# Two post-norm transformer layers on one core: weight loads on another queue, two sets of split parts, row maxima through an fp32 transpose, and new orders

## The reference, cut to what matters

```python
x = _layernorm(x + _L0_attn_ref(x, L0_attn_w_project, L0_attn_w_out), axis=-1)
x = _layernorm(x + _L0_ffn_ref(x, L0_ffn_gate_w, ..., L0_ffn_down_s), axis=-1)
x = _layernorm(x + _L1_attn_ref(x, L1_attn_Wq, ..., L1_attn_bo), axis=-1)
x = _layernorm(x + _L1_ffn_ref(x, L1_ffn_W_up, L1_ffn_W_gate, L1_ffn_W_down), axis=-1)
# attention, 16 heads of 16, causal:
att = jnp.einsum('bhqd,bhkd->bhqk', q, k) / math.sqrt(HEAD_DIM)
att = jax.nn.softmax(jnp.where(causal, -1e9, att), axis=-1)
out = jnp.einsum('bhqk,bhkd->bhqd', att, v)
# expert (ternary_quant: scale = mean|W|, clip(round(W/scale), -1, 1) * scale):
hidden = jax.nn.silu(x @ wu.T) * (x @ wg.T);  y = hidden @ wd.T
```

## Time and profile before

| | |
|---|---|
| median of 3 runs | 284.59 us |
| profiled execution | 287.4 us, of which the span is 285.7 |
| TensorE busy | 253.5 us (89%), mean granted clock 0.933 |
| VectorE busy | 222.5 us (78%) |
| GpSimd busy | 162.1 us (57%) |
| ScalarE busy | 153.6 us (54%) |

### The profile page before, as it was taken

The page is one execution under the profiler, slowest core; times in us unless marked ns, Lnnn a source line. Parts: engine busy times, 40 slices in busy tenths (PEclk is TensorE's granted clock), DMA queues, the critical chain, the costliest instruction groups (busy, mean ns, idle before and its releaser), DMA issues.

```text
span 285.7 us, 6810 instructions
## 1 busy us (share of the span) xinstructions
PE 253.5 (89%) x2396; PEld 221.3 (77%) x2396; DVE 222.5 (78%) x833; ACT 153.6 (54%) x284; POOL 162.1 (57%) x171
## 2 busy tenths in 40 slices
PE   1997646899999999999999898798999999999991
PEld 1897323467789999989999796676779888999980
DVE  1746999888967466853888999999998987888674
ACT  3634315567773524593634447657777765425440
POOL 9966235785550416443293796685651796645371
PEclk9999755569999999999999999799999999999996
DMA  6997556182000000016173029135021000010101
GB/s 212 319 247 195 170 158 175 37 262 79 6 0 2 2 0 5 0 35 191 44 201 127 1 61 262 51 87 139 7 83 67 5 0 2 2 39 0 39 1 73
DMA packets 18898, 24.18 MB, mean 85 GB/s; under 512 B 2480, under 2 KB 17328, under 8 KB 18224
## 3 DMA queue, kind: packets, MB, share of 16 engines
q1 hardware_dynamic: 18048, 22.95, 27.8%
q10 hardware_dynamic: 816, 0.79, 1.0%
HBM read 9.97 MB, written 1.05 MB: 39 GB/s over the span
## 4 chain that ended last, share of the span: by engine, by line
PE 55%; DVE 14%; DMA 8%; issue 7%; POOL 7%; SPq 4%; ACT 4%; POOLq 0%; DVEq 0%; ACTq 0%
PE pair L484 7%; PE pair L485 6%; PE pair L486 6%; PE pair L565 6%; PE pair L632 5%; PE pair L633 4%; SPq L461 4%; PE pair L548 4%; POOL k_stack L981 4%; PE pair L529 3%; PE pair L568 2%; PE pair L575 2%; DMA raw<-f0gu 2%; DMA raw<-f0dn 2%; PE pair L654 2%
## 5 line engine op out<-in xcount | busy, mean ns | idle before, releaser
L1013 POOL TENSOR_SCALAR_AFFINE_SELECT probs<-probs 128x512 f32<-128x512 f32 x64 | 42.6, 671 | 40.3 <-ACT probs L721 39.2
L1029 POOL TENSOR_TENSOR hidden<-hf,hidden 128x512 fp32r<-128x512 f32 x28 | 36.1, 1290 | 42.8 <-ACT hidden L763 42.7
L873 DVE CUSTOM_DVE_ANT_0 masked<-pair,mask 128x256 bf16<-128x256 f32 x128 | 53.5, 418 | 7.5 <-PE pair L530 7.3
L721 ACT ACTIVATE probs<-pair 128x768 f32<-128x768 f32 x64 | 49.2, 814 | 15.1 <-PE pair L550 12.9
L876 DVE CUSTOM_DVE_ANT_0 masked<-pair,mask 128x128 bf16<-128x128 f32 x128 | 36.4, 284 | 0.0
L936 DVE SCALAR_TENSOR_TENSOR hf<-th,pair 128x512 f32<-128x512 f32 x28 | 19.2, 685 | 20.2 <-ACT th L752 11.8
L529 PE MATMUL pair<-k_stack,q_stack 96*128 96x256 bf16 x128 | 30.7, 305 | 4.5 <-DVE row_max L876 2.3
L548 PE MATMUL pair<-q_stack,k_stack 98*128 98x256 bf16 x128 | 28.7, 294 | 4.4 <-DVE row_max L876 2.3
L763 ACT ACTIVATE hidden<-hf 128x512 fp32r<-128x512 f32 x28 | 17.7, 631 | 20.2 <-DVE hf L939 15.4
L484 PE MATMUL pair<-xT_hi,gu_hi 128*128 128x256 f32 x96 | 27.6, 288 | 1.0 <-DVE hf L939 1.0
L530 PE MATMUL pair<-k_stack,q_stack 96*128 96x128 bf16 x128 | 27.4, 239 | 0.0
(11 more groups left out here) (136 smaller groups left out, 844.0 us busy)
## 6 DMA issues: line engine op xcount, KB each, us to landing
q_stack<-q_part SPq DMA_DIRECT2D x48, 128.0 KB, 2.4
k_stack<-k_part SPq DMA_DIRECT2D x48, 128.0 KB, 2.5
raw<-f SPq DMA_DIRECT2D x3, 1024.0 KB, 5.4
raw<-f0gu SPq DMA_DIRECT2D x2, 768.0 KB, 5.9
x<-x_nat SPq DMA_DIRECT2D x1, 1024.0 KB, 8.1
raw<-a SPq DMA_DIRECT2D x1, 1024.0 KB, 5.0
out<-x SPq DMA_DIRECT2D x4, 256.0 KB, 2.2
probs<-x_tr SPq DMA_DIRECT2D x3, 256.0 KB, 5.9
```

The lines of the kernel that those rows point to most:

```text
L721: nc.scalar.activation(probs[(n - 1) % 4][:, :, :], place(key)[:, :, 0:T + P], ACT.Exp, scale=SC).then_inc(exp_done, 1)
L873: nc.vector.tensor_tensor_reduce(out=masked[:, j, 0:T], in0=o[:, 0:T], in1=mask[:, 0:T], scale=1.0, scalar=NEG, op0=ALU.add, op1=ALU.max, ...
L1013: pool.affine_select(out=diag, in_=diag, compare_op=ALU.is_ge, fill=0.0, base=0, pattern=[[0, 2], [0, 2], [1, P]], channel_multiplier=-1). ...
L1029: pool.tensor_tensor(hidden[(n - 1) % NHID][1][:, :, :], hf[n % 2][:, :].rearrange("p (a t) -> p a t", a=2), hidden[(n - 1) % NHID][0][:, ...
```

## The change

1. The -1 rows of the k stacks are written as fp32 words that each hold two bf16 values of -1.
2. SP's first loads are ordered anew, and the load of `x_nat` is issued behind batch 0's stack transfers. The seven later loads into `raw` become steps RAW on ScalarE, each with the wait it had on SP.
3. There are two sets of the q/k parts, taken in turn, so ScalarE waits only for the transfers of the batch before the last.
4. Row maxima: TensorE transposes `row_max` itself in fp32 (padded to 128 columns), ScalarE copies 16 rows as the high part, VectorE subtracts to get the low part, and SP writes them with two transfers (MX and ML) instead of one.
5. All five orders and the bank table are written anew, and `shift` is kept in `bo_b`.

```diff
+MINUS_PAIR = struct.unpack("<f", struct.pack("<I", 0xBF80BF80))[0]
...
 SYNC_STEPS = """
-    LOAD:001-2 LOAD:000 QK:000 PREPA:003 MID:000 LO:000 MID:001 QK:001 LO:001 QK:010 MID:010 QK:011 PREP0:001
+    LOAD:000-1 QK:000 MID:000 LO:000 QK:001 LO:001 MID:001 LOAD:002 QK:010 MID:010 QK:011 LO:010 QK:020-1 LO:011
...
-        part_of = [[sb(f"{name}_part{n}", [P, 2 * T], bf16) for n in range(3)] for name in "qk"]
+        part_of = [[[sb(f"{name}_part{n}_{m}", [P, 2 * T], bf16) for n in range(3)] for name in "qk"] for m in range(2)]
...
             load_a0(sp, 0)
-            for b in range(1, NB):
-                load_x(sp, b)
+            load_a0(sp, 1)
+            load_x(sp, 1)
+            load_a0(sp, 2)
+            load_x(sp, 2)
+            load_x(sp, 3)
             load_a0(sp, 3)
...
+                if step in ("MX", "ML"):
+                    n = nth("MX", l, b)
+                    row, done, part = (KP, maxT_hi_done, maxT_hi) if step == "MX" else (KP + 1, maxT_done, maxT_lo)
+                    sp.wait_ge(done, n)
+                    sp.dma_start(q_stack[nb_of(l, b) % SLOTS][row:row + 1, :, :].rearrange("p h t -> p (h t)"),
+                                 part[n % 2][:, :]).then_inc(max_rows[n % 2], 16)
...
                 if step == "MX":
-                    pe.wait_ge(max_split, nth("MX", l, b))
+                    pe.wait_ge(max_taken, 2 * nth("S", l, b, NS - 1))
...
-                        last = nc.tensor.matmul(o[:, qt * P:(qt + 1) * P], max_hl[:, qt, :],
-                                                ident_b[:, :], start=True, stop=True)
+                        last = nc.tensor.transpose(o[:, qt * P:(qt + 1) * P], row_max[b % 2][:, qt, :], ident[:, :])
...
         def _(act):
             load_x(act, 0)
-            load_a0(act, 1)
-            load_a0(act, 2)
...
+                if step == "RAW":
+                    if i == 0:
+                        act.wait_ge(wa0_lo, 4)
+                        act.dma_start(raw[:, 0:2 * W0], f0gu[:, 0, :]).then_inc(raw_in, 16)
+                    if i == 1:
+                        act.wait_ge(w_lo, 2)
+                        act.dma_start(raw[:, 0:2 * W0], f0gu[:, 1, :]).then_inc(raw_in, 16)
...
+                    if i == 4:
+                        act.wait_ge(w_lo, PREP0 + PREP1)
+                        act.dma_start(raw[:, :], f1[:, 0, :]).then_inc(raw_in, 16)
...
-                    for q in before_of(l, b):
-
+                    if nb_of(l, b) > 1:
+
+                        q = batches[nb_of(l, b) - 2]
                         act.wait_ge((q_stacked, k_stacked)[i][nb_of(*q) % SLOTS], stacked_by(*q))
...
-                    rm = row_max[b % 2]
-                    nc.vector.tensor_copy(max_hl[:, :, 0:H], rm[:, :, :]).then_inc(max_hi, 1)
-                    dve.wait_ge(max_hi, n)
-                    nc.vector.tensor_tensor(max_hl[:, :, H:2 * H], rm[:, :, :], max_hl[:, :, 0:H],
-                                            ALU.subtract).then_inc(max_split, 1)
+                    dve.wait_ge(maxT_hi_done, n)
+                    nc.vector.tensor_tensor(maxT_lo[n % 2][:, :], place(key)[0:H, 0:T], maxT_hi[n % 2][:, :],
+                                            ALU.subtract).then_inc(maxT_done, 1)
...
-                pool.memset(k_stack[n][KP:KP + 2, :, :], -1.0).then_inc(minus_rows, 1)
+                pool.memset(k_stack[n][KP:KP + 2, :, :].bitcast(fp32), MINUS_PAIR).then_inc(minus_rows, 1)
```

More of the change, by code:

```diff
@@ L221, in program @@
         ident = sb("ident", [P, P])
-        ident_b = sb("ident_b", [P, P], bf16)
         mask = sb("mask", [P, 384])
@@ L249, in program @@
         masked = sb("masked", [P, 2, T + P], bf16)
-        row_max = [sb(f"row_max{n}", [P, 2, H]) for n in range(2)]
-        max_hl = sb("max_hl", [P, 2, 4 * 2 * H], bf16)
-        maxT = sb("maxT", [2 * H, T], bf16)
+        row_max = [sb(f"row_max{n}", [P, 2, P]) for n in range(2)]
+        maxT_hi = [sb(f"maxT_hi{n}", [H, T], bf16) for n in range(2)]
+        maxT_lo = [sb(f"maxT_lo{n}", [H, T], bf16) for n in range(2)]
         probs_all = sb("probs", [P, 4 * 2 * (T + P)])
@@ L292, in program @@
         k_stacked = [sem(f"k_stacked{n}") for n in range(SLOTS)]
-        max_rows = sem("max_rows")
+        max_rows = [sem(f"max_rows{n}") for n in range(2)]
         stored = sem("stored")
@@ L696, in _ @@
                     act.wait_ge(qk_left, nth("SPLIT", l, b, i))
-                    nc.scalar.activation(part_of[i][1][:, :], left[i][:, :], ACT.Copy).then_inc(qk_mid, 1)
+                    nc.scalar.activation(part_of[nb_of(l, b) % 2][i][1][:, :], left[i][:, :], ACT.Copy).then_inc(qk_mid, 1)
                 if step == "V":
@@ L853, in _ @@
                         dve.wait_ge(qk_lo, k_ - 2)
-                    src, first = place(key), part_of[i][0]
+                    src, first = place(key), part_of[nb_of(l, b) % 2][i][0]
                     if l == 0:
@@ L865, in _ @@
                         dve.wait_ge(consts, 6)
+                    if i == 0 and nth("MX", l, b) > 2:
+                        dve.wait_ge(mx_mm, nth("MX", l, b) - 2)
                     for j in range(2):
@@ L980, in _ @@
             for n in range(SLOTS):
-                pool.memset(k_stack[n][KP:KP + 2, :, :], -1.0).then_inc(minus_rows, 1)
+                pool.memset(k_stack[n][KP:KP + 2, :, :].bitcast(fp32), MINUS_PAIR).then_inc(minus_rows, 1)
             pool.wait_ge(minus_rows, SLOTS)
             pool.memset(ones[:, :], 1.0).then_inc(consts, 1)
-            pool.memset(ident_b[:, :], 0.0).then_inc(pool_own, 1)
             pool.memset(minus_half[:, :], -0.5)
-            pool.memset(max_hl[:, :, 2 * H:4 * 2 * H], 0.0).then_inc(consts, 1)
+            for n in range(2):
+                pool.memset(row_max[n][:, :, H:P], 0.0).then_inc(consts, 1)
             pool.memset(ident[:, :], 0.0).then_inc(pool_own, 1)
             pool.memset(mask[:, :], 0.0).then_inc(pool_own, 1)
-            pool.wait_ge(pool_own, 3)
-            pool.affine_select(out=ident_b[:, :], in_=ident_b[:, :], compare_op=ALU.not_equal, fill=1.0, base=0,
-                               pattern=[[-1, P]], channel_multiplier=1).then_inc(consts, 1)
+            pool.wait_ge(pool_own, 2)
             pool.affine_select(out=ident[:, :], in_=ident[:, :], compare_op=ALU.not_equal, fill=1.0, base=0,
```

170 lines of the change are left out of this document (79 added, 91 removed), and 16 rows, old and new, of the table BANKS.

## The result

The changed kernel takes 295.39 us (294.1 to 298.0), the one before on the same chip 285.1 us (284.52 to 286.16): ratio 1.0337, 95% interval 1.0284 to 1.0391. I had forecast 279.1 and at most 285.5. The profiled execution took 296.58 us, 294.8 of it span.

The account below looks back on a forecast made before the run. VectorE was taken to set the pace to about 55 us, PE after it. Gains of 3.5 us in the start and 2.0 in layer 1, together 5.5, took 284.6 to 279.1 us, range 274.3 to 285.5.

Parts of the forecast that it names:

- -1 rows: GpSimd's start: memsets as fp32 pairs fall from 10.40 to 5.2 us, visible gain 2.3 us; 0 if time goes by bytes.
- x late: Start: x_nat's load issued behind batch 0's stacks costs nothing, as its reader comes tens of us later.
- Loads on ScalarE: Seven weight loads moved from SP cost ScalarE's queue about 0.6 us each, 4 in all; taken 0, bound 4.
- My rival: Slower: a layer-1 weight load in ScalarE's order delays batch (1,1)'s k split, PE idles 4 us; 288.1 us, chance 0.1.
- Batch 1's stacks: Start: 20 SP issues, 13 us, about 1 us of waits to 32.5, 2.5 us to land: there at 35.0.
- VectorE's 37.0: Start: VectorE begins batch 1's maxima at 37.0 against 38.31, 1.3 us earlier.
- My own sign for a wrong forecast: Start: the forecast is wrong if batch 1's stacks keep VectorE idle past 38 us.
- Row maxima: VectorE: 9.4 us of small operations removed, 8 subtractions of 0.41 added, 3.3 us; 6.1 saved, bounds 0.8 and 8.0.
- The clock: Start: PE's granted clock, which rose at 62.8 us, is back at 1.0 between 56 and 60.
- Layer 1: Less VectorE work and perhaps no half-clock stretch at 182 us: 2.0 us gained, bounds -3 and +4.
- The rule on issuing engines: Loads from another engine share 16 DMA engines, saving only issue time; cited for the rival without a lead, 283.6, chance 0.15.
- the small sum: Moving seven loads off SP is worth about seven issues of 0.6 us there and no faster landing.

Follow-up runs that it names:

- after_x_early: The changed kernel with SP issuing the x_nat load ahead of batch 0's stack transfers instead of behind them: 296.21 us, 1.0353 to the kernel before.
- after_queues_untied: The changed kernel with ScalarE's second gate/up load and SP's last k parts of batch 1 issued ahead of the waiting batch 2 k copy: 291.91 us, ratio 1.0149.
- after_light_loads: The changed kernel with layer 1's three feed-forward weight loads carrying 16 columns instead of 2048: 293.58 us, ratio 1.0259 to the kernel before.

## Why the prediction was wrong

- **-1 rows.** Size right: 5.28 us, taken 5.2. Their 2.3 us at S:000 came as 1.2 in the whole change; alone they moved the end by nothing that can be told. I had S:000 start at 22.7 behind ScalarE's copies. These and VectorE's subtraction were through by 21.4, but batch 0's stacks were not: SP had issued them by 17.86 (18.3 taken), the k transfers took 5.3 us in the median and not 2.5, and PE started S:000 at 23.24.
- **x late: nothing.** At the end it costs no more than early (after_x_early). But it fills the DMA engines beside batch 1's stacks, which I left out of their landing time.
- **Loads on ScalarE: taken 0.** Too low for the old orders (1.6% gained alone), and in the new orders a step failed here: I worked out when the first gate/up load goes out and never when the second does. It stands behind QK:021's copy, and that behind PE's 2.81 us stall for batch 0's stacks, three scores and 12 products at half clock: 28.13 us. I had ScalarE free of that wait; it stood 6.03 us for PE and 4.17 for the load. My rival said that ScalarE is in order and any of the seven waits could do it, and then priced only the one at 145 us, which did no harm (PE was busy 24.69 of 25 us in 150 to 175).
- **Batch 1's stacks: 35.0. This is the step that failed first.** I counted 20 issues and "about 1 us of waits". SP waited 1.9 us for QK:021 and was through these 20 at 34.1, not 32.5. One of the last, from 33.53, took 6.59 us to land, not 2.5: 40.1. Of the 5.1 us, 4.1 are the landing, which I had taken from the median of the earlier trace rows over the whole kernel, and 1.0 the queue. From there VectorE's 37.0 became 41.88. Why the landing was long is shown only in part: the DMA engines were full from 18 to 38 us (1.09 against 0.74), with `x_nat`, the slipped load and batch 2's parts in flight. With `x_nat` moved away the transfer took 4.30 us (after_x_early); the other two were never taken away by themselves. What is shown is that issuing batch 1's parts and the load ahead of the copy gives 1.9% back (after_queues_untied). My own sign for a wrong forecast, VectorE idle for these stacks past 38, came true.
- **Row maxima: 6.1 us saved.** A saving is there, if smaller (busy 4.0 us less when done alone; 7.8 in the whole change, beside other differences), and the subtraction takes 0.41 as estimated, all eight times. But I priced it as VectorE time and not as a link: PE, ScalarE, VectorE, SP and a transfer now follow one another, 2% slower and not faster. This is the second failed step.
- **The clock.** The long half-clock stretch does end sooner (56.4 against 62.8), as forecast. But it is no longer alone: there are three short ones, 6.8 + 6.7 + 6.8 us, each begun while PE stood idle (2.81, 2.65 and 1.93 us), where the kernel before had one of 3.5 at 182 us.
- **Layer 1: +2.0.** PE idles 4.82 us in 175 to 205 and not 3.39. The load at 175.29 goes out with batch (1,2)'s stacks behind it, some 0.8% (after_light_loads, not clear of its interval).
- **The rule on issuing engines** (the Trainium skill, DMA: Bandwidth & Descriptors, section Issuing engines are not separate DMA queues): loads issued by another engine share the same 16 DMA engines, so moving them saves issue time. The landings agree with the sharing: in the new orders a q stack transfer takes 5.7 us in the median with the loads on ScalarE and 5.1 with them on SP. At the end of the kernel the small sum held in one case of three: moving the seven loads alone gave 1.6%, about 4.5 us, where their issues on SP are some 4; in the new orders it is worth 2.0% (1.0543 against 1.0337), with the changed operations and the old orders nothing (1.0130 and 1.0137). So the issue time saved does not fix what the end gains; the order around the loads matters as well.

The sum of the parts closes within the intervals: 0.9844 for the loads, 2.0% for the maxima and 0.6% for the three others (0.5 - 0.3 + 0.4, each within its interval of nothing) make 1.010, measured 1.0137; the start's orders add 2.0%. Left open is why the new order behind the start, whose waits on PE are others, does no better and no worse than the old one.

## What to carry to other kernels

When instructions trade places, walk every in-order queue and ask what stands behind each waiting instruction, loads and DMA issues above all: one copy that waited 6 us for its product held back a weight load and the next batch's transfers, and moving those two past it was worth 1.9%. An operation that gets cheaper but now waits for two other engines has become a link: price the chain, not the busy time. And take a transfer's landing time from rows where the same neighbours are in flight.

## What the runs showed of the hardware

- A 128 KB transfer from SBUF to SBUF took 2.4 us to land in the median of the kernel before. With the DMA engines full (share 1.09 from 18 to 38 us) those of the changed kernel took up to 7.8 us, 6.59 in the chain. In layer 1 they took 6.1 us (q) and 4.9 (k) in the median beside a 1 MB load and 2.4 without it (after_light_loads). Which engine had issued the loads made little difference: 5.7 us with them on ScalarE, 5.1 with them on SP.
- GpSimd's memset goes by elements and not bytes: 4096 bf16 in 3.47 us each, the same bytes as 2048 fp32 in 1.76 (three took 10.40 and 5.28).
- At 70.2 and 186.1 us PE was granted half clock for 6.7 and 6.8 us, and both times the fall came inside a single wait, of 2.65 and 1.93 us. In the 4.16 us before the first wait PE was busy 3.92 us, in the 10.45 us before the second 8.19. Where the second wait was gone (after_light_loads) the clock stayed at 1.0.
